# First and quantised attention: other orders at their beginnings and ends, and filling products in their ramps

## The reference

```python
x = x + L0_attn(layernorm(x))          # gated + causal attention, mixed, then a third attention on the mix
x = x + L0_xattn(layernorm(x), ctx)    # one head, 77 context tokens
x = x + L0_ffn(layernorm(x))           # 8 routed experts (top 2) + 2 shared, gelu
x = x + L1_attn(layernorm(x))          # quantised attention, 16 heads of 8
x = x + L1_xattn(layernorm(x), ctx)    # 16 heads, then a two-layer relu net
x = x + L1_ffn(layernorm(x))           # 16 routed experts (top 2) + shared, silu

# L1_attn: fake_quant rounds to 256 levels between min and max
xq, wq = fake_quant(x, axis=-1), fake_quant(qkv_w, axis=0)
q, k, v = split(xq @ wq.T + qkv_b)
attn = softmax(fake_quant(q) @ fake_quant(k).T * scale)
out = attn @ fake_quant(v)
return fake_quant(out) @ fake_quant(proj_w, axis=0).T + proj_b
```

## Time and profile before

| | |
|---|---|
| median of 3 runs | 687.2 us (686.75 to 687.46) |
| the profiled execution, its own time | 685.16 us |
| its span | 683.4 us |
| busy: PE, DVE, ACT, POOL | 580.7, 418.8, 383.9, 94.7 us |
| share of the span: PE, DVE, ACT, POOL | 85%, 61%, 56%, 14% |
| mean granted clock of TensorE | 0.924 |

### The profile page before, as it was taken

How to read it: one execution, slowest core, us unless ns; L and a number is a source line. 1 busy time by engine, 2 the same in 40 slices (tenths; PEclk the granted TensorE clock), 3 DMA queues, 4 the chain that set the end, 5 groups by cost and what they waited for, 6 DMA issues and landing times. The chain is left out here.

```text
span 683.4 us, 9372 instructions
## 1 busy us (share of the span) xinstructions
PE 580.7 (85%) x3281; PEld 316.6 (46%) x3281; DVE 418.8 (61%) x859; ACT 383.9 (56%) x684; POOL 94.7 (14%) x99
## 2 busy tenths in 40 slices
PE   2379899988999687999999997478988766998997
PEld 1112233322343444889998994211222234645876
DVE  8268577577741553635663335887999346746674
ACT  2246866667667247657655441245989723685631
POOL 8200200100000001700000000299000003000000
PEclk9759999999999998999999996568999979997999
DMA  5324210444070700200000000000000001000000
GB/s 159 92 35 60 67 28 2 62 63 64 2 290 23 89 1 20 102 0 2 0 1 1 14 2 1 0 0 2 2 1 2 1 0 71 27 4 1 1 17 15
DMA packets 14785, 22.68 MB, mean 33 GB/s; under 512 B 3524, under 2 KB 9908, under 8 KB 14356
## 3 DMA queue, kind: packets, MB, share of 16 engines
q1 hardware_dynamic: 12916, 15.54, 11.5%
q10 hardware_dynamic: 1824, 6.55, 2.5%
HBM read 9.99 MB, written 0.52 MB: 15 GB/s over the span
## 5 line engine op out<-in xcount | busy, mean ns | idle before, releaser
L536 DVE TENSOR_REDUCE negmax<-ps 128x2 f32<-128x1024 f32 x96 | 113.9, 1221 | 40.9 <-PE ps L467 40.4
L583 ACT ACTIVATE probs<-ps 128x512 f32<-128x512 f32 x192 | 105.9, 598 | 38.6 <-PE ps L486 36.7
L583 ACT ACTIVATE probs_q<-ps,score_scale 128x512 f32<-128x512 f32 x128 | 78.1, 687 | 14.6 <-PE ps L486 13.1
L1858 PEld LDWEIGHTS ps<-experts,hid 128*128 128x128 f32 x640 | 82.6, 191 | 6.9 <-issue 1.0
L1858 PE MATMUL ps<-experts,hid 128*128 128x128 f32 x640 | 84.0, 275 | 0.0
L536 DVE TENSOR_REDUCE negmax_q<-ps 128x2 f32<-128x1024 f32 x64 | 74.8, 1219 | 6.0 <-PE ps L467 5.5
L1935 ACT ACTIVATE hid<-ps 128x512 f32<-128x512 f32 x80 | 47.0, 598 | 47.8 <-PE ps L864 47.8
L864 PE MATMUL ps<-experts,wfc 128*128 128x512 f32 x156 | 49.3, 424 | 0.0
L467 PE MATMUL ps<-gated 64*128 64x512 bf16 x128 | 29.2, 427 | 20.3 <-DMA gated<-parts 9.3
L2029 DVE SCALAR_TENSOR_TENSOR x_tok<-ps,comb,x_tok 128x128 f32<-128x128 f32 x64 | 18.0, 344 | 43.1 <-PE ps L1858 43.1
L500 PE MATMUL ps<-probs_q,v_q 128*32 128x512 f32 x256 | 43.1, 672 | 0.0
(11 more groups left out here) (383 smaller groups left out, 920.9 us busy)
## 6 DMA issues: line engine op xcount, KB each, us to landing
q_wide<-parts SPq DMA_DIRECT2D x12, 256.0 KB, 5.7
k_wide<-parts SPq DMA_DIRECT2D x12, 256.0 KB, 7.1
experts<-in_L_ffn_Wfc_dram ACTq DMA_DIRECT2D x1, 2560.0 KB, 9.1
experts<-in_L_ffn_Wproj_dram ACTq DMA_DIRECT2D x1, 2560.0 KB, 15.7
gated<-parts SPq DMA_DIRECT2D x18, 128.0 KB, 2.4
qs_x<-crossing SPq DMA_DIRECT2D x5, 256.0 KB, 3.0
w<-in_L_ffn_W_dram SPq DMA_DIRECT2D x1, 1024.0 KB, 5.5
square_weights<-in_squares_dram SPq DMA_DIRECT2D x1, 768.0 KB, 7.1
```

The costliest lines, as they stand in the source:

```text
L536: nc.vector.tensor_reduce(maxima, scores, AX.X, ALU.max, negate=True).then_inc(self.a_max_done, 1)
L583: nc.scalar.activation(self.probs[0:size, g % self.P_SLOTS, :], ps[0:size, self.B_BANK + g % self.B_SLOTS, :], ACT.Exp, scale=scale).then_ ...
L1858: last = nc.tensor.matmul(K.ps[:, y_bank(g), i * P:(i + 1) * P], hid[:, m % SLOTS, i * P:(i + 1) * P], wproj[:, FT * e + f, :], start=(f = ...
```

## The change

1. *Semaphores.* `recycle` and its barriers go; `release` clears a stage's semaphores at the start of the next stage's code (POOL does it), with no barrier of its own.
2. *Start of first attention.* Half 0 alone is transposed and projected; half 1's transposes come after the values item. 22 products of the identity stand first, 4 filling products before the first projection, 20 after the prologue. The cuts of the first key and query move from POOL to VectorE (`prologue_vector`), the copy of `h_ft` of half 1 and the wait for POOL's constants behind them; ScalarE's first cast moves ahead of the query item. POOL sets `v_wide` before `v16` and waits for all normalisation before the latter.
3. *Ramps.* After each of nine `A` steps (`RAMP`) in both attentions two filling products (`G`); ten before the first `A` of quantised attention; one after every second unit from unit 105 in its tail.
4. *End of first attention.* The product with `mc_Wout` for half 1 moves from the experts' block to the stage's end, between 4 and 6 filling products; ScalarE's load of the sigmoid table moves ahead.
5. *Start of quantised attention.* The bias product of values of half 0 moves to the experts' end; ranges of q and v are taken by half, with one small reduction after them.
6. *End of quantised attention.* All that follows the attention moves into the block of cross attention (`QuantOutputs`), whose steps for half 0 no longer stand behind those of half 1; POOL's constants of that block then run beside it. 3 filling products, not 6, before the first `A`, and 8 at the end of cross attention.

```diff
-    def recycle(self, keep=()):
-
-        done = [n for n in self.made if n not in keep]
-        self.nc.all_engine_barrier()
-        self.nc.clear_and_free_semaphores([self.made.pop(n) for n in done])
-        self.nc.all_engine_barrier()
+    def release(self, names):
+
+        self.nc.clear_and_free_semaphores([self.made.pop(n) for n in names])
...
+RAMP = [("A", 0, 2), ("A", 0, 3)] + [("A", 1, i) for i in range(4)] + [("A", 2, i) for i in range(3)]
...
+    def prologue_vector(self, dve, item):
+
+        K, nc, stk = self.K, self.K.nc, self.stk
+        if item == 0:
+            stk.cut_rest(dve, nc.vector, 0)
+        elif item == 2:
+            stk.dve_read(dve, 2)
+            stk.cut_last(dve, nc.vector, 0)
+            stk.cut_rest(dve, nc.vector, 1)
+        elif item == 3:
+            stk.cut_last(dve, nc.vector, 1)
+            dve.wait_ge(*self.cleared)
+            stk.dve_read(dve, 3)
+            dve.wait_ge(self.ln.turned, NT)
+            nc.vector.tensor_copy(K.h_ft[:, HALF:2 * HALF], K.ps[:, self.ln.banks[1], :]).then_inc(self.ln.h_by_dve, 1)
...
-    extras["end"].append(("X", 0, X.FIRST))
-    prologue += [(kind, n, 0) for kind in "QL" for n in range(PROLOGUE)]
+    extras["end"] += [("K", 4, 7), ("W", 1, 0), ("K", 6, 7), ("X", 0, X.FIRST)]
+    prologue[2:2] = [("Q", 0, 0)]
+    prologue += [("Q", 2, 0), ("L", 0, 0), ("L", 2, 0)]
+    prologue.append(("G", 20, GatedAttention.FILL_BANK))
+    for step in RAMP:
+        extras["after", step] = [("G", 2, Attention.O_BANK)]
...
+            clear_v(nc.gpsimd, filled, v4, 32)
+            filled(nc.gpsimd.memset(K.inv[:, :], 1.0))
+            pool.wait_ge(ln.xn_ready, NT)
             clear_v(nc.gpsimd, filled, v16, 8)
-            clear_v(nc.gpsimd, filled, v4, 32)
-            nc.gpsimd.memset(K.inv[:, :], 1.0).then_inc(made_v, 1)
...
-                if m == 0:
-                    nc.tensor.matmul(K.ps[:, 6, :], W["L0_attn_mc_Wout"][:, :], ft_a[:, meta], start=True, stop=True) \
-                        .then_inc(n["meta_done"], 1)
...
             next_ln.turn(pe, 1)
+            pe.wait_ge(next_ln.h_ready, 1)
+            Q.bias_of_values(K, 0)
...
-    att = QuantAttention(K, "attq", jobs, 2, 8, *attention_buffers(sb, "q", st), evacuate_on_vector=True,
-                         busy=(0, 0, 1))
+    extras = {("after", step): [("G", 2, 0)] for step in RAMP}
+    att = QuantAttention((n["v_scaled"], 2), K, "attq", jobs, 2, 8, *attention_buffers(sb, "q", st), evacuate_on_vector=True,
+                         extras={**extras, **{g: [("K", 1, 1)] for g in range(105, 128, 2)}},
+                         busy=(10, 0, 1))
...
+    def ends_by_half(dve, a, done):
+        for b in range(NB):
+            dve.wait_ge(done, b + 1)
+            product = K.ps[:, BANK[a] + b, :]
+            chain(nc.vector.tensor_reduce(half_ends[:, 0, a, b:b + 1], product, AX.X, ALU.min, negate=True))
+            chain(nc.vector.tensor_reduce(half_ends[:, 1, a, b:b + 1], product, AX.X, ALU.max))
...
-    extras["end"] = [("Y", 0, tail.RAW), ("Y", 0, tail.LOW)]
-    att = HeadsAttention(tail, K, "attx", jobs, 4, 6, *attention_buffers(sb, "x", st), extras=extras, busy=(6, 2, 7))
+    extras["end"] = [("Y", 0, tail.RAW), ("Y", 0, tail.LOW), ("K", 8, 7)]
+    att = HeadsAttention(tail, K, "attx", jobs, 4, 6, *attention_buffers(sb, "x", st), extras=extras, busy=(3, 2, 7))
...
         @block.tensor
         def _(pe):
+            outputs.spread_range(pe)
             keep_busy(K, 6, 6)
-            ln.tensor(pe)
             for b in range(NB):
-                ln.wait_half(pe, b)
+                outputs.turn(pe, b)
+            keep_busy(K, 6, 1)
+            for b in range(NB):
+                outputs.project(pe, b)
+            keep_busy(K, 6, 6)
+            for b in range(NB):
+                ln.turn(pe, b)
+                pe.wait_ge(ln.h_ready, b + 1)
                 interleaved(nc, K.ps[:, 4 + b, :], W["L1_xattn_Wq"], K.h_ft[:, half(b)], STRIP_SIDES) \
                     .then_inc(s["projected"][b], 1)
...
         @block.vector
         def _(dve):
-            ln.vector(dve)
+            outputs.find_range(dve)
+            for b in range(NB):
+                outputs.ints(dve, b)
+            outputs.out_second(dve)
+            outputs.add(dve, 0)
+            ln.stats(dve, 0)
+            outputs.add(dve, 1)
+            ln.normalise(dve, 0)
+            ln.stats(dve, 1)
+            ln.normalise(dve, 1)
```

More of the change, by code:

```diff
@@ new lines, in cut_rest @@
+    def cut_rest(self, eng, ops, m):
+        n = self.cut[m]
+        it = self.items[n]
+        slot, cols = m % self.slots, it["cols"]
+        full, rest = self.full[:, slot, 0:cols], self.rest[:, slot, 0:cols]
+        eng.wait_ge(self.part1_done, m + 1)
+        if it.get("gated"):
+            eng.wait_ge(self.f_by_dve, self.number(n, lambda x: x.get("gated")))
+        else:
+            eng.wait_ge(self.f_by_act, self.number(n, lambda x: x["kind"] in "qk" and not x.get("gated")))
+        if it["parts"] == 2:
+            ops.tensor_tensor(self._part(n, 1), full, as_f32(self._part(n, 0)), ALU.subtract) \
+                .then_inc(self.rest_done, 1)
+        else:
+            ops.tensor_tensor(rest, full, self._part(n, 0), ALU.subtract).then_inc(self.rest_done, 1)
```

220 lines of the change are left out of this document (130 added, 90 removed).

## The result

The changed kernel takes **680.6 us** (median of 4 runs, 678.06 to 681.12), the kernel before 687.0 beside it: ratio 0.9898, 95% interval 0.9867 to 0.9928, so 6.4 us faster where 21.6 were forecast. The profiled execution took 680.74 us, span 679.0, mean clock 0.931 (before 685.16, 683.4 and 0.924), so the sum of terms is compared with -4.4 us of span. From here on a time is the median of all runs of a kernel, which lie up to 34 us apart, with the lowest and highest in brackets, while a ratio, with its 95% interval, leaves out the runs over 1.5% above their kernel's fastest, such as the 703 us among those of the kernel before.

A forecast was written before the change was run, and what follows sets the result against it. In the attention ramps no engine was taken as full: VectorE and TensorE wait for each other at low clock. Terms a to i sum to -21.6 us, giving 665.6 us against the 687.2 median; range 659 to 674.

The forecast's parts named there:

- a: Start of first attention: earlier projection and gated query bring the first score product to 24.6 us, -6.5 us.
- b: Ramp of first attention: filling products behind nine score blocks, full clock shortens the stage, -2.5 us (range 0 to 5).
- c: End of first attention and start of the experts: TensorE starts the experts at full clock, -2.5 us.
- d: Experts to quantised attention: two all-engine barriers and the semaphore clearing go or move to idle POOL, -2.0 us.
- e: Start of quantised attention: bias product moved ahead, reductions on halves, half the ten products' possible cost taken off, -0.5 us.
- f: Ramp of quantised attention: the same nine pairs, VectorE loses perhaps half of 8.6 idle us at full clock, -2.5 us.
- rival 2: Slower: filling products run at half clock on the path in ramps, tail and both ends, +6.3 us, 693; 4%.
- Rival 1: The clock falls in the ramps all the same; b, f and g are zero: -15.1 us, 672; 28%.
- g: Tail of quantised attention: twelve single products keep TensorE fuller against clock dips, -1.5 us.
- h: Output of quantised attention joined to cross attention: half 0's work no longer waits for half 1, -3.6 us.
- rival 3: VectorE and POOL exclude each other in the output range: -19.0 us, 668; 10%.
- i: Eight products at the end of cross attention: 0 us, ends +2.5 and -1.5.

The follow-up runs named there:

- the orders alone: The changed kernel with all added identity and weight products taken out, only the new orders and missing barriers left: 673.0 us, ratio 0.979.
- the first of the four kernels of that group: The changed kernel without the nine pairs of the quantised ramp and with GpSimd's constants late: 670.7 us, ratio 0.9764.

## Why the prediction was right and wrong

The sign was right, the size was not: -6.4 us instead of -21.6, outside the range. By its own terms:

- **a** is -8.2 (31.16 to 22.96) instead of -6.5: 5.1 from the earlier start (4.8 in the sum), 1.1 behind the projections (1.6), and 2.0 from the projections themselves (nothing). The step that failed in it is "the 22 products at the start gain nothing of themselves", since the trace had "full clock in the first slice". The same projections take 4.83 us before, 5.36 with the orders alone, 4.37 without the identity products and 2.80 with them, with 1.00 printed for the clock in all. That 1.00 was misread. The traces have no record of the clock ahead of 20.1 us before, of 15.3 in the two kernels without identity products and of 5.2 with them; each record begins there with full clock, and the views print 1.00 where there is none. The Trainium skill (TensorE: Matmul & The Clock Gate, Part 1) has half rate as the default that activity lifts; durations and first records agree, and the 2.4 us that the prediction estimated by it came out as 2.0. That the kernel with the orders alone meets the forecast 24.6 with 24.57 is partly luck: it starts 1.0 us earlier, as the four filling products are out, and loses 0.5 in the projections and 0.3 behind them.
- **b** is -1.7 instead of -2.5 (30.32 to 28.63 us), and its reason fell: the clock was higher (0.89 against 0.74 with the orders alone), and the ramp was no shorter for it (28.63 against 28.55 us). So the 1.7 is not shown to be the products', and its nearness to 2.5 is luck; why the orders alone shorten the ramp by 1.8 was not tried.
- **c** is -1.2. The experts' first product comes 8.1 us after the last transposes instead of 6.0, so it is 2.1 later and not 0.9: the clock fell at 261.2, just ahead of the first of the ten products (261.67), and four of them and the moved product ran at half. In the second execution of the same kernel the clock stayed full there, and the 8.1 is 6.5.
- **d** and **e** held: -2.0, and -1.1 with the ten products hidden, which is the term without the half microsecond that it took off for them.
- **f** is the step that failed most: "at full clock it would lose perhaps half of these 8.6 idle us". It took the pairs to keep the clock, for which no row of this ramp spoke. The clock fell 3 us after the first block, a block and a pair took 1.70 us (1.59 was worked out under rival 2) against VectorE's 1.15, and the ramp lost 5.1 us. Rival 1 had this clock right but put the pairs at nothing. Rival 2 got 4% because it was priced for ramps, tail and both ends at once; in one ramp alone it needed a case of its own.
- **The steady part** was in no term. TensorE works there for 50 of 57 us at full clock, and at half it is the bound: 17 us at half clock cost 5.4 (62.3 against 56.9), 34 cost 10.9, 51 cost 16.3, so 0.32 us for each. All six profiled executions with one, two or four products behind a ramp block, and none at the passage, have such a stretch (17, 17, 34, 34, 51 and 51 us); of the eight without products behind the ramp's blocks one has it (51), and the others 3.4 us or none. The kernel before is not free of it for certain: of its 48 runs on record 43 lie at 684.6 to 687.8 us and one at 690.8, but four take 696.8 to 703.1, with 36 to 57 us more at low clock than its profiled execution, by their mean clocks, and some 0.3 us lost for each. None of the four was traced.
- **g** is -0.6 instead of -1.5. The clock stayed at 1.00 through the tail (0.85 before), so what was too large is the 3.2 us put on the dips. It repeats: the tail takes 21.46 or 21.47 us in all thirteen traces with the twelve products, 22.03 to 22.14 in the three without.
- **h** is -0.4 instead of -3.6, and 1.8 of that is rival 3. It had been set aside by the earlier trace rows, one subtraction of 0.68 us beside a short select; here two additions and a tiny instruction stood beside three long selects. The row was also misread. These lines of GpSimd stand around the select in it, kernel before:

```profile
276.33 0.29 POOL L1668 TENSOR_SCALAR_AFFINE_SELECT strip_rows<-strip_rows 128x16 f32<-128x16 f32 x1
277.27 0.21 POOL L1672 TENSOR_SCALAR_AFFINE_SELECT strip_rows<-strip_rows 128x16 f32<-128x16 f32 x1
```

VectorE's subtraction began first (276.44 to 277.12), the select of the row came second (276.68) and took 0.52 us where its like take 0.21 to 0.29, so the row can be read for the exclusion, with GpSimd as the one that waits. It is not clean: the select at 276.33 had begun before the subtraction and did not lengthen it. The Trainium skill (SBUF — State Buffer, Who interferes with whom) states the exclusion; the runs agree (1.8 us, where 2.6 at most was worked out). With the constants late, this stretch is 1.7 to 3.2 us shorter than before. The rest was not separated: transposes, projections and filling ran at half clock until 564.9 and from 571.8 us on, 17 us of this stretch against 10 before.
- **i** is -2.1, and that is not shown to be the products'. With the eight products the last stretch takes 86.3 us in eight traces, where the clock falls in it only at the very end, and 87.9 to 89.1 in five with a dip of 3.4 to 6.8 us ahead of the last experts, the same program among them (87.9). With the orders alone, which have no such products, it takes 86.6 with a dip of 3.4 us (609.2 to 612.6).
- **First attention** lost 3.5 us in dips at 141, 227 and 240 us that no term had. The first, 1.5 us, is chance: the same program did not have it again. The others are not only that. All thirteen profiled executions of kernels with the filling at the start have a dip between 220 and 250 us and take 204.4 to 209.8 us for this stretch; the three without the filling (before, before with the pairs, orders alone) have none and take 203.5 or 203.6. So 0.9 us at the least seems to come with the filling. How, and with which of the products, is open; it is there without the 22 identity products too.
- Two smaller readings: the steps listed under h add up to 576.55 and not 576.7, and the "50 us of cross attention" at full clock under rival 1 are 44.4 in the trace (576.4 to 620.8).

Missed to the slow side: f 7.6, steady part 4.2, first attention 3.5, h 3.2, c 1.3, g 0.9; to the fast side: i 2.1, a and b 0.9, e 0.6. Together 17.1, the distance from -21.6 to the -4.5 that the rounded rows of the table add up to.

**Open:** what starts and ends the half clock of the steady part. With four products in the ramp and 16 at the passage none of five runs had it, with six there two of seven, and the first of the four kernels of that group, with no products at either place, has one run of six that looks like it; so few runs don't show that the 16 prevent it. That TensorE's waits at the passage are what makes the clock fall is only argued.

## What to carry to other kernels

Price a filling product at half clock first: it is free only where block and filling together stay under the other engine's step (here 0.61 + 0.98 us stood against 1.15), and too little filling costs the path without holding the clock. Read the clock at the start from the durations of like products, not from a printed share. Where a steady stage uses TensorE for most of its time (here 50 of 57 us), a fall of the clock can make it the bound, so look there for the price of what is changed ahead of it. When GpSimd's work is moved beside a chain of VectorE, take its longest instructions as the price, not one short row, and look which of the two began first in that row.

## What the runs showed of the hardware

- Being busy did not by itself bring the clock back: TensorE worked 7.00 of 7.00 us at clock 0.50, on 32-row score products and products with the probabilities, and in stretches of 51 us (50.85 us busy with one product and with four).
- Some dips belong to the execution: the same program ran at half clock from 141.7 to 145.1 us in one execution and at full in the next, 1.5 us apart behind it. Others recur: one between 220 and 250 us in thirteen of thirteen traces with filling at the start, in none of three without.
- A clock printed as 1.00 at the start was no measure of TensorE's rate (5.36 against 2.80 us for the same products): the records of the clock began only at 15.3 and at 5.2 us.
- A VectorE instruction on 2 x 2 elements took 0.81 us beside GpSimd's selects and 0.22 without them.
